# A kernel of four conditioned layers: arrival counts for gathered expert weights, and the order and size of the first loads

## What is computed

```python
# L0: down projection, expert of the sequence, up projection, layer norm
hidden = gelu(einsum('bsd,ad->bsa', x, down_W) + down_b)
hidden = einsum('bsa,boa->bso', hidden, expert_W[idx]) + expert_b[idx] + domain_emb[idx]
x = layernorm(hidden @ up_W.T + up_b + x) * ln_gamma + ln_beta
# L1: scale and shift from silu(sin_emb(timestep)) @ W_ada + b_ada
x = ln(x) * (1.0 + scale) + shift
x = x + attention(x, bias=attention_bias, mask=src_mask) @ Wo + bo
x = x + gelu2((ln(x) * g2 + beta2) @ W1 + b1) @ W2 + b2
# L2: weights of 512 KB (Wi and Wo together) for each sequence, picked by expert_idx
h = gelu(einsum('bsh,bhi->bsi', x, Wi[expert_idx]) + bi[expert_idx])
r = einsum('bsi,bih->bsh', h, Wo[expert_idx]) + bo[expert_idx] + x
x = norm(r) * gamma[expert_idx] + beta[expert_idx]
# L3: causal attention block, then the gate
x2 = block(x)
return x + gate_score * (x2 - x)
```

## Time and profile before

| | |
|---|---|
| median of 3 runs | 193.13 us (192.99 to 193.62) |
| profiled execution, first to last instruction | 192.6 us |
| busy: PE, DVE, ACT, POOL | 146.7, 133.2, 111.8, 89.2 us |
| moved by DMA | 31.43 MB, mean 163 GB/s |

### The profile page before, as it was taken

The page is one execution under the profiler, slowest core; times in us unless marked ns, Lnnn a source line. Parts: engine busy times, 40 slices in busy tenths (PEclk is TensorE's granted clock), DMA queues, the critical chain, the costliest instruction groups (busy, mean ns, idle before and its releaser), DMA issues.

```text
span 192.6 us, 4924 instructions
## 1 busy us (share of the span) xinstructions
PE 146.7 (76%) x1598; PEld 109.9 (57%) x1598; DVE 133.2 (69%) x400; ACT 111.8 (58%) x273; POOL 89.2 (46%) x137
## 2 busy tenths in 40 slices
PE   7399943806357478799899897685978989898884
PEld 7067812404244247697577666463647577787673
DVE  4356844409087685958665769599699999996724
ACT  2083562302105233695999969796376666888781
POOL 0021532904444668899632443226638687453210
PEclk9958555755857958999999999999699999999999
DMA  3996245644528837976977686877994422011001
GB/s 45 307 401 219 32 121 162 155 131 137 133 64 231 249 65 231 325 232 180 254 229 239 174 242 219 245 198 254 240 220 153 118 63 73 14 45 54 27 5 41
DMA packets 23688, 31.43 MB, mean 163 GB/s; under 512 B 3350, under 2 KB 18007, under 8 KB 23664
## 3 DMA queue, kind: packets, MB, share of 16 engines
q1 hardware_dynamic: 23394, 31.06, 56.1%
q10 hardware_dynamic: 270, 0.07, 0.2%
HBM read 28.50 MB, written 1.57 MB: 156 GB/s over the span
## 4 chain that ended last, share of the span: by engine, by line
SPq 30%; DMA 20%; DVE 17%; PE 14%; issue 14%; ACT 3%; POOL 0%; DVEq 0%; ACTq 0%
DMA selv<-in_eout 16%; SPq L541 9%; SPq L530 6%; SPq L532 4%; SPq L529 4%; SPq L517 4%; DMA hg<-in_experts 4%; DVE nrm L859 2%; PE bank L660 2%; PE bank L655 2%; DVE mx L893 2%; PE bank L571 2%; PE bank L594 2%; DVE sc L885 2%; PE bank L629 1%
## 5 line engine op out<-in xcount | busy, mean ns | idle before, releaser
L1007 POOL TENSOR_TENSOR vbd<-vrep,tab 128x512 f32<-128x512 f32 x16 | 17.1, 1069 | 15.2 <-DMA vrep<-vdram 11.6
L728 ACT ACTIVATE lnv<-mv,eps 128x1 f32<-128x1 f32 x48 | 13.9, 290 | 17.3 <-DVE mv L850 16.9
L999 POOL TENSOR_TENSOR qbd<-qkt,tab 128x512 f32<-128x512 f32 x16 | 18.2, 1137 | 11.5 <-DVE qkt L875 7.2
L629 PEld LDWEIGHTS bank<-kex,qbd 128*128 128x128 f32 x128 | 20.3, 225 | 1.8 <-issue 1.0
L629 PE MATMUL bank<-kex,qbd 128*128 128x128 f32 x128 | 20.1, 309 | 0.0
L557 PE MATMUL bank<-tab,res 128*128 128x128 f32 x16 | 5.5, 346 | 18.5 <-DVE res L865 18.5
L750 ACT ACTIVATE hg<-bank,tab 128x128 f32<-128x128 f32 x64 | 18.0, 382 | 2.7 <-PE bank L655 2.4
L618 PE MATMUL bank<-tab,xt 128*128 128x384 f32 x32 | 18.0, 658 | 1.9 <-DVE xt L855 0.9
L859 DVE TENSOR_SCALAR nrm<-res,mv,rstd 128x128 f32<-128x128 f32 x40 | 18.3, 465 | 1.3 <-ACT rstd L730 1.3
L655 PE MATMUL bank<-xt,tab 128*128 128x128 f32 x128 | 17.4, 280 | 1.5 <-DVE xt L855 1.2
L660 PE MATMUL bank<-tab,hg 128*128 128x128 f32 x128 | 17.4, 281 | 1.3 <-ACT hg L750 1.3
(11 more groups left out here) (124 smaller groups left out, 354.4 us busy)
## 6 DMA issues: line engine op xcount, KB each, us to landing
wexp<-in_wexp SPq DMA_DIRECT2D x32, 512.0 KB, 3.7
vrep<-vdram SPq DMA_DIRECT2D x64, 64.0 KB, 3.0
fm<-in_fside SPq DMA_DIRECT2D x8, 256.0 KB, 4.8
tab<-in_tab SPq DMA_DIRECT2D x2, 768.0 KB, 9.7
selv<-in_eout SPq DMA_DIRECT2D x32, 48.0 KB, 4.2
adav<-emb SPq DMA_DIRECT2D x8, 128.0 KB
vdram<-qkv SPq DMA_DIRECT2D x16, 64.0 KB, 3.4
rows<-in_rows SPq DMA_DIRECT2D x1, 768.0 KB, 8.0
```

The costliest lines, as they stand in the source:

```text
L629: mm = pe.matmul(ps[:, g * P:(g + 1) * P], qbd[:, k, g].rearrange("p b s -> p (b s)"), kex[:, k, g].rearrange("p h s -> p (h s)"), start=F ...
L728: link(act.activation(lnv[:, t:t + 1], mv[:, t, 1:2], ACT.Ln, bias=eps[:, 1:2] if layer == "e" else eps[:, 0:1]))
L999: ins = pool.tensor_tensor(qbd[:, k], qkt[:, k, 0, :, None, :].broadcast_to([P, HG, NB, S]), tab[:, None, at:at + NB, None].broadcast_to([ ...
L1007: ins = pool.tensor_tensor(vbd[:, k].rearrange("p b g w -> p (b g) w")[:, :, 0:H4 * DH].rearrange("p n (h d) -> p n h d", h=H4), vrep[:, k ...
```

## The change

Three things are changed. The expert pieces get four semaphores, one for each sequence of a tile; SP waits ahead of wl_b(t) only until wl_b(t-1) has landed, and e1 and xbo2 wait for all four. Of the first loads, `cvec` takes in `down_wt` and the two masks (72 columns, 36 KB, instead of 32 columns, 16 KB), so that `tab0` is the identity alone; `experts0` goes as 16 rows and 1 row; `xt` goes as tiles 0 and 1 (128 KB), then the rest (384 KB). The waits follow: down(0) on `cvec` and the first part of `xt`, down(2) on the rest, the mask steps on `cvec`, the first transposes tr_b(0) and tr_d(0) on `tab0`.

```diff
@@ -448,12 +448,12 @@
         loaded = {n: sem("loaded_" + n) for n in
-                  ("xt", "x", "cvec", "tab0", "tab_ada", "tab1", "tab3", "rows", "experts0", "idx0", "idx1",
+                  ("xt", "xt_rest", "x", "cvec", "tab0", "tab_ada", "tab1", "tab3", "rows", "experts0", "idx0", "idx1",
                   "idx2", "up33", "ada_b", "evec2",
...
         landed = {n: [sem(f"landed_{n}_{k}") for k in range(SLOTS)] for n in TRANSFERS}
-        wl_landed = [sem("wl_even_landed"), sem("wl_odd_landed")]
+        wl_landed = [sem(f"wl_landed_{b}") for b in range(NB)]
         idle_ready = sem("idle_ready")
@@ -465,8 +465,7 @@
-                piece = t * NB + int(name[-1])
-                eng.wait_ge(wl_landed[piece % 2], 32 * (piece // 2 + 1))
+                eng.wait_ge(wl_landed[int(name[-1])], 32 * (t + 1))
                 return
@@ -489,10 +488,13 @@
             at = COL["cvec"][0]
-            sp.dma_start(tab[:, at:at + 32], a["tab"][:, at:at + 32]).then_inc(loaded["cvec"], 16)
-            sp.dma_start(experts0, a["experts0"]).then_inc(loaded["experts0"], 16)
-            sp.dma_start(xt[:].rearrange("p t s -> p (t s)"), a["xt"]).then_inc(loaded["xt"], 16)
-            sp.dma_start(tab[:, 0:at], a["tab"][:, 0:at]).then_inc(loaded["tab0"], 16)
+            first = COL["down_wt"][0]
+            sp.dma_start(tab[:, first:at + 32], a["tab"][:, first:at + 32]).then_inc(loaded["cvec"], 16)
+            sp.dma_start(experts0[0:E0], a["experts0"][0:E0]).then_inc(loaded["experts0"], 16)
+            sp.dma_start(experts0[E0:E0 + 1], a["experts0"][E0:E0 + 1]).then_inc(loaded["experts0"], 16)
+            sp.dma_start(xt[:, 0:2].rearrange("p t s -> p (t s)"), a["xt"][:, 0:2 * P]).then_inc(loaded["xt"], 16)
+            sp.dma_start(xt[:, 2:NT].rearrange("p t s -> p (t s)"), a["xt"][:, 2 * P:NT * P]).then_inc(loaded["xt_rest"], 16)
+            sp.dma_start(tab[:, 0:first], a["tab"][:, 0:first]).then_inc(loaded["tab0"], 16)
             sp.dma_start(tab[:, at + 32:t1], a["tab"][:, at + 32:t1]).then_inc(loaded["tab_ada"], 16)
@@ -508,7 +510,7 @@
                     reuse(sp, name, t)
-                    sig = landed[name][k] if name in landed else wl_landed[int(name[-1]) % 2]
+                    sig = landed[name][k] if name in landed else wl_landed[int(name[-1])]
                 if name == "ada":
@@ -522,10 +524,8 @@
                         sp.wait_ge(done["w_oh2"], 1)
-                    if b > 1:
-                        arrived(sp, f"wl{b - 2}", t)
-                    elif t > 0:
-                        arrived(sp, f"wl{b + 2}", t - 1)
+                    if t > 0:
+                        arrived(sp, name, t - 1)
                     e = sp.value_load(eidx[0:1, t * NB + b:t * NB + b + 1], min_val=0, max_val=E2 - 1)
@@ -565,7 +565,7 @@
-                    pe.wait_ge(loaded["experts0"], 16)
+                    pe.wait_ge(loaded["experts0"], 32)
                     pe.wait_ge(done["w_oh0"], 1)
@@ -589,8 +589,10 @@
                     if t == 0:
-                        pe.wait_ge(loaded["tab0"], 16)
+                        pe.wait_ge(loaded["cvec"], 16)
                         pe.wait_ge(loaded["xt"], 16)
+                    if t == 2:
+                        pe.wait_ge(loaded["xt_rest"], 16)
                     mm = pe.matmul(ps[0:A, 0:P], col("down_wt"), xt[:, t, :], start=True, stop=True)
@@ -606,6 +608,8 @@
                 elif name in ("tr_b", "tr_d"):
+                    if t == 0:
+                        pe.wait_ge(loaded["tab0"], 16)
                     pe.wait_ge(done["aff_b" if name == "tr_b" else "res2"], t + 1)
@@ -661,8 +665,8 @@
                     pe.wait_ge(done["ev_d"], t + 1)
-                    arrived(pe, "wl2", t)
-                    arrived(pe, "wl3", t)
+                    for b in range(NB):
+                        arrived(pe, f"wl{b}", t)
                     for b in range(NB):
@@ -876,7 +880,7 @@
                     if t == 0:
-                        dve.wait_ge(loaded["tab0"], 16)
+                        dve.wait_ge(loaded["cvec"], 16)
                     dve.wait_ge(done["qkt3"], t + 1)
@@ -959,7 +963,7 @@
-                    pool.wait_ge(loaded["tab0"], 16)
+                    pool.wait_ge(loaded["cvec"], 16)
                     ins = pool.tensor_copy(
@@ -1018,8 +1022,8 @@
                     pool.wait_ge(done["res2"], t + 1)
-                    arrived(pool, "wl2", t)
-                    arrived(pool, "wl3", t)
+                    for b in range(NB):
+                        arrived(pool, f"wl{b}", t)
                     ins = pool.tensor_tensor(resb[:, t, :], res[:, t, :], selv[:, t, 0:D], ALU.add)
```

## The result

The changed kernel takes 184.97 us (median of 4 runs, 184.30 to 185.31), the kernel before, run beside it, 193.38 us (192.99 to 193.89). The ratio is 0.957, with a 95% interval of 0.951 to 0.964: 8.4 us faster, where 185.1 was forecast.

A forecast was written before the change was run, and what follows sets the result against it. Until some 124 us the path was taken to run through the transfers, not an engine's arithmetic. Span 192.6 - 2.7 - 2.4 - 2.9 = 184.6, plus 0.5 for the median gives 185.1 us; range 182.0 to 189.0.

The forecast's parts named there:

- Part 1: At the start, experts and timesteps land earlier, so ada(0) is issued at 13.5 instead of 16.19 us: -2.7 us.
- Part 2: Four counts, 30 to 60 us: wl2(0) and wl3(0) issued at once, so ada(3) lands earlier: -2.4 us.
- Part 3: Four counts, 100 to 140 us: SP's waits for pieces go, engines regain lost time: -2.9 us, bounds 0 and -6.1.
- lower bound of -4.5: At the start: the most ada(0) could gain, with DVE no longer last and PE straight through.
- SP is held in the issue itself: At wl2(0), 30 to 60 us: if a full queue holds SP anyway, removing the wait gains 0.
- e1(5): Late stretch: PE's step starts up to 1.06 us earlier and DVE waits for it next: -1.1 us.
- xbo2(4): Late stretch: POOL's step starts up to 3.22 us earlier, of which DVE had lost 0.8: -0.8 us.
- third term: Late stretch: vr3(0) issued some 3 us earlier frees vbd3(0), qbd3(1) and PE's wait: -1.0 us.
- rival that ended slower: At ada(3), vr3(0), vr3(1): small transfers wait behind two more pieces, +2.8 us net, 195.9 us; chance 0.08.
- Only the early parts count: Late stretch gains nothing because PE, ACT and DVE are short of time themselves: 188.0 us; chance 0.14.
- no change: Over the whole kernel, smaller pieces cost three added landings, 5.1 us against 5.3 gained: 193 us; chance 0.05.
- More: Late stretch reaches the full bound of its gain: 181.9 us; chance 0.10.

The follow-up runs named there:

- halves of the columns: Kernel before, with the 17 expert rows loaded as two transfers that halve the columns, each still 17 rows: 194.72 us against 194.26, ratio 1.005.
- copies spread in four: Each ada copy as four transfers, one for each sequence: 188.20 us (ratio 0.974) in the kernel before, 181.03 us in the changed kernel.
- counts alone: Kernel before with the four semaphores and their waits, loads as they were: 189.56 us against 194.35, ratio 0.976.
- counts and split: Kernel before with the four counts and the experts as 16 rows and 1 row, without the pieces of `xt` and `cvec`: 186.75 us, ratio 0.969.
- changed with 17 rows: Changed kernel with `experts0` again as one transfer of 17 rows: 189.58 us, ratio 0.976.
- late waits back: Changed kernel with the old waits put back for tiles 4 to 7 only: 186.08 to 192.55 us in 4 runs, too wide for a ratio.
- late counts alone: Kernel before with four semaphores, the old waits kept for tiles 0 to 3: 192.10 us against 194.26, ratio 0.989.
- changed kernel once more: Changed kernel, unaltered, measured again on another chip against the kernel before: 184.92 us against 194.01, ratio 0.953.
- row split alone: Kernel before with, of the new loads, only the experts as 16 rows and 1 row: 189.51 us, ratio 0.972.
- changed kernel spread in four: Changed kernel with each ada transfer as four, each spreading one row of `emb`: 181.03 us against 184.92 of the changed kernel.

## Why the prediction was right, point by point

The total was right, 185.1 against 184.97, and so were the mechanisms of parts 1 and 2. That it came so close is partly luck: part 1 was some 2 us too small and part 3 over 1 us too large, and the two errors cancel.

**Part 1, -2.7.** The cause was right: 17 rows in one transfer were what PE waited for. The row count decides, as the halves of the columns show. The Trainium skill's rule (DMA: Bandwidth & Descriptors, "Why a DMA increments its semaphore by 16 and not by 1") puts 17 rows on one engine. At the 31 / (0.21 x 16) = 9.2 GB/s that a busy engine moves in the earlier trace rows, one would need 8.0 us for the 72 KB (an estimate), and in the kernel before they were there 7.0 us after their issue at 1.18 in SP's timeline. But a busy engine moves anything from 3.8 to 25 GB/s in the windows of this document, so that one engine carries the 17 rows is not shown.

The size was off by the timesteps. They were guessed at 6.2 us, though they are read at 4.35 in the changed kernel. The forecast's own path with this number gives 4.35 + 4.5 + 0.1 + 0.9 + 1.06 + 0.72 = 11.6, and ada(0) was issued at 11.51: DVE was done at 8.8 and not at 10.7, and PE waited for it. In the two other profiles in which PE starts fast, DVE is last too (PE waits 1.02 and 1.15 us for it), and ada(0) is at 10.98 and 10.80. In the other five profiles with the split PE ran at half that speed from w_sel on; there PE is last, and ada(0) is at 13.47. That this is the forecast's 13.5 is a coincidence. So the term is -2.7 or about -5. The lower bound of -4.5 was too near as well, because it took PE's steps from the one speed of the trace of before.

**Part 2, -2.4.** Confirmed in size, and in place by the kernels that differ in these waits alone. Counts that go free early shorten the stretch from ada(0) to wl0(4) by 2.7 us. Giving back only the two waits of tile 0 makes it 83.7 us, against 80.6 and 81.4 in the two kernels without early waits whose ada(0) is also at 13.47. From the issue of ada(0) to DVE's aff_b(3) pass 24.8 to 28.0 us in the six kernels with the early waits (mean 26.7) and 22.9 to 25.6 in the six profiles without them (mean 24.5), copies spread in four left out: 2.2 less. wl2(0) comes 1.6 us after wl1(0), as forecast, in four kernels (counts alone, counts and split, changed with 17 rows, late waits back), but not in the changed kernel itself, where it takes 3.08 and 4.87 us. There SP is held by its own issues, and what holds it are the spread copies of ada(0) to ada(2): with these in four the same issues take 0.33 us and wl2(0) comes after 1.60. The bound "SP is held in the issue itself" was half right.

**Part 3, -2.9.** Over-estimated, by about 1: 1.6 (2.1 with the marked traces) by the stretches, and 2.2 (interval 1.0 to 3.5) by the time of the late counts alone. In the trace of the changed kernel the whole stretch gained only 1.1. Of its terms, e1(5) gave the 1.0 that was taken as 1.1. xbo2(4) gave nothing of its 0.8: it starts 9.0 us earlier than before where wl0(4), at the head of the series, is issued 9.1 earlier. The forecast took SP's wait for the whole delay; but a piece that is issued sooner behind its neighbours also lands later, 4.9 us instead of 3.2. The third term, -1.0 for vr3(0), failed: the copies are issued 12.1 us earlier and serve 9.3 us earlier, only 0.2 us more than the 9.1 by which wl0(4) is earlier. That is the mechanism of the rival that ended slower. At vr3(0) it is real, 1.4 us a copy in the median, and it was priced far too high: two pieces of 2.63 us at each of three places. At ada(3) it doesn't show: from its issue to aff_b(3) pass 7.0 us in the kernel before and in the changed one.

**The signs.** Of the signs of being right, w_sel, the wait for ada(3) (4.07 us, over at 34.37 and so sooner than 38.5) and the spacing of wl0(4) to wl3(5) came true. wl2(0) 1.6 us after wl1(0) did not, nor did xbo2(4) without a wait (2.88 and 1.90 us in the two profiles). One sign of being wrong appeared in the first of the two, the longer POOL wait for `vrep`.

**The offset.** The forecast put the median 0.5 us above the profiled span. In all later runs a run takes 2.1 to 2.2 us more than its span (184.63 and 182.4), so the profiled execution of before must have taken some 194.8 us (an estimate, 192.6 + 2.2), against a median of 193.1. This explains why the spans differ by 10.2 and the medians by 8.4. It did no harm: span and median were lowered by the same 8.0.

**The sum of the parts.** At PE's half speed the terms give -2.7 - 2.7 - 1.6 = -7.0, at its full speed -4.7 - 2.7 - 1.6 = -9.0; measured were 8.4 and, beside the changed kernel once more, 9.1, both with PE fast in the profile. The times of single edits add up less well: by their ratios the counts alone gave 4.7 us and the row split alone 5.5, but both together 6.0 (3.7 to 8.2). Why is open. *Only the early parts count* (188.0) is refuted in the kernel before by the late counts alone, whose interval excludes nothing gained. *More* (181.9) and *no change* (193) lie outside of all eight runs of the changed kernel (183.70 to 190.13). *No change* counted three added loads where the change adds two, so by its own price of 1.7 us each it stood at 191.2. The 2 us that it quotes from the Trainium skill are given there (DMA: Bandwidth & Descriptors, "Anatomy of one DMA — SWDGE (gpsimd) path") for transfers issued from GpSimd; those here come from SP, and the first landed in 1.7 us. What the forecast missed altogether is that the spread copies themselves were the next thing to mend, although it had named their engines as the bottleneck.

## What to carry to other kernels

Look at the row count of each transfer that stands at the head of a kernel: one row too many (17 instead of 16) cost 3 us here, and halving the bytes instead cured nothing. Where small copies that spread a few rows stand ahead of large loads and the DMA share is far below one (0.21 here) though SP is held in its next issues, try them row by row: splitting them by row was worth as much (3.9 and 5.1 us) as rewriting the counts. Before a wait is taken away, ask what then lands later behind the larger number in flight: here the small row copies, and the pieces themselves. Price terms of 1 to 3 us from several traces, as one kernel's own stretches differ by 2 us.

## What the runs showed of the hardware that was not expected

**TensorE starts at either of two speeds.** The same w_sel, starting at 4.94 us (4.66 in the changed kernel spread in four), takes 2.18, 1.90 and 1.87 us in three profiles and 3.61 or 3.62 in five; ten matmuls of the downs take 1.28 us, 0.13 each, or fourteen 3.19, 0.23 each. The warm-up matmuls ahead of it show no difference between the changed kernel and counts and split: their last ten take 1.27 us from 3.73 in both. In the changed kernel the granted clock falls from full towards half behind the first downs, and the four that follow take 1.03 us, 0.26 each, and w_emb 1.06. Its windows (columns as in rows 5):

```profile
5.00:10.00 5.00, 4.56 (x24) 2.46 (x24) 3.50 (x16) 3.46 (x6) 0.50 (x2) 0.90 1.04 333
10.00:15.00 5.00, 5.00 (x54) 4.00 (x52) 3.22 (x15) 2.53 (x7) 0.85 (x1) 0.50 1.00 396
```

And those of counts and split, where PE is slow from w_sel on:

```profile
5.00:10.00 5.00, 5.00 (x16) 2.00 (x16) 4.11 (x17) 2.27 (x4) 0.78 (x3) 1.00 1.01 336
10.00:15.00 5.00, 5.00 (x41) 3.81 (x39) 1.86 (x8) 2.61 (x8) 0.85 (x1) 1.00 1.01 396
```

Here the column says 1.00 (2.4 GHz), but w_emb takes 1.06 us as it does at 0.50 (1.2 GHz) in the changed kernel, and the fourteen matmuls take the 3.19 us that they take at 0.50 in the kernel before. So at the start the column can't be trusted and the duration of a known matmul is the better gauge. It is worth 2.0 to 2.7 us at ada(0). The three profiles that start fast all have the small pieces of `xt`, but so do three of the five slow ones; what decides it stays open. No kernel was seen at both speeds: both profiles of the changed kernel start fast, and every other kernel has one profile.

**More engines on a spread copy, little more rate.** Split by row, the copies of ada hold 0.80 of the DMA engines instead of 0.21, and move 48 GB/s instead of 31: 3.8 GB/s for a busy engine instead of 9.2. In the queue the issues of wl0(0) and its `selv` take 0.36 and 0.34 us there, against 2.63 and 2.79 before, but the twelve issues of ada(0) to ada(2) take 8.78 us instead of 6.07 for three; wl1(0) is issued 1.4 us sooner. The larger gain comes later, at qkvb1(3), 3.8 us. What bounds the rate of such a copy, if not the count of engines, was not measured.
